# Order within a block of a three-layer graph attention kernel: sums before turnings, weighting before older residuals, first feed-forward product ahead of the next block

## What is computed

```python
for l in range(2):                       # layers 0 and 1
    xn = layernorm(h)
    q, k, v = xn @ wq[l] + bq[l], xn @ wk[l] + bk[l], xn @ wv[l] + bv[l]
    scores = einsum('ehd,ehd->eh', q[dst], k[src]) * scale
    ex = exp(scores - segment_max(scores, dst)[dst])
    agg = segment_sum((ex / segment_sum(ex, dst)[dst])[:, :, None] * v[src], dst)
    h = h + agg @ wo[l] + bo[l]
    h = h + gelu(layernorm(h) @ w1[l] + b1[l]) @ w2[l] + b2[l]
# layer 2 ("typed"): keys are K[src] + 0.2 * rel_w[edge_type]; no feed-forward part
x = layernorm(agg @ Wo + bo + node_features) * gamma + beta
```

## Time and profile before

| | |
|---|---|
| median of 3 runs | 6028.8 us (6025.58 to 6051.66) |
| the profiled execution | 6041.55 us, of which its span is 6039.4 us |
| mean granted TensorE clock | 0.742 of full |
| busy in the span | PE 3256.9 us (54%), DVE 3499.7 us (58%), ACT 1879.4 us (31%), POOL 2782.5 us (46%) |
| layers 0, 1 and typed | about 640 to 2590, 2590 to 4580 and 4580 to 6039 us |

### The profile page before, as it was taken

One profiled execution on the slowest core, in us unless ns is written; L12 is line 12 of the kernel. 1 busy time (PEld: TensorE's weight loads), 2 busy tenths in 40 slices (PEclk: granted clock), 3 DMA queues, 4 the chain that ended last, 5 costly groups with the idle time before them and its releaser, 6 DMA issues. The chain is left out here.

```text
span 6039.4 us, 88354 instructions
## 1 busy us (share of the span) xinstructions
PE 3256.9 (54%) x17373; PEld 2423.7 (40%) x17374; DVE 3499.7 (58%) x5216; ACT 1879.4 (31%) x4257; POOL 2782.5 (46%) x2783
## 2 busy tenths in 40 slices
PE   8575455455555555635545454455565545555655
PEld 6232334333333344523433343333344434444444
DVE  6441445545555555544555555555554758798887
ACT  3342232222222233323222222223334423334444
POOL 0330444544444444244454544444424557777664
PEclk9786677677777777867767777777787767666667
DMA  3343545545455444355554545544434546666654
GB/s 122 120 153 75 160 141 148 158 143 152 140 148 149 143 138 137 102 160 153 149 167 143 158 135 148 152 141 144 138 107 137 162 136 181 183 185 186 176 175 127
DMA packets 369280, 886.73 MB, mean 147 GB/s; under 512 B 140773, under 2 KB 153279, under 8 KB 369225
## 3 DMA queue, kind: packets, MB, share of 16 engines
q0 software_dynamic: 217200, 702.54, 40.3%
q1 hardware_dynamic: 151708, 182.79, 9.4%
q10 hardware_dynamic: 320, 0.84, 0.0%
HBM read 742.87 MB, written 143.30 MB: 147 GB/s over the span
## 5 line engine op out<-in xcount | busy, mean ns | idle before, releaser
L1283 POOL DMA_INDIRECT kv<-kv_dram,idx x2430 | 2421.5, 997 | 1121.8 <-issue 722.1
L2085 PE MATMUL ps_w<-w_ffn,shared 128*128 128x256 f32 x1568 | 567.9, 539 | 1423.8 <-ACT shared L1816 1326.9
L2085 PEld LDWEIGHTS ps_w<-w_ffn,shared 128*128 128x128 f32 x1568 | 432.0, 283 | 1559.5 <-ACT shared L1816 1367.3
L1411 DVE TENSOR_REDUCE sc<-products 128x32 f32<-128x1024 f32 (+2 forms) x654 | 784.3, 1211 | 17.2 <-DVE products L1404 11.8
L1991 PE MATMUL ps_acc<-ident,kv 128*128 128x128 f32 x4944 | 701.9, 305 | 49.0 <-issue 40.0
L1519 DVE TENSOR_TENSOR kv<-kv,ps_q 128x1024 f32<-128x1024 f32 x594 | 683.9, 1215 | 4.5 <-issue 0.3
L1991 PEld LDWEIGHTS ps_acc<-ident,kv 128*128 128x128 f32 x4944 | 645.1, 159 | 96.9 <-issue 69.6
L1816 ACT ACTIVATE shared<-ps_big,b 128x128 f32<-128x128 f32 x784 | 214.6, 380 | 1462.2 <-remote 1444.9
L1404 DVE TENSOR_TENSOR products<-kv,ps_q 128x1024 f32<-128x1024 f32 x436 | 523.4, 1219 | 52.1 <-issue 42.4
L1251 POOL DMA_INDIRECT kv_dram<-rec_out,scatter_to x98 | 100.3, 1024 | 849.3 <-issue 849.3
L2072 PE MATMUL ps_big<-xnaT,w_ffn 128*128 128x128 f32 x3136 | 393.4, 280 | 106.0 <-issue 102.1
(11 more groups left out here) (243 smaller groups left out, 5367.7 us busy)
## 6 DMA issues: line engine op xcount, KB each, us to landing
rec_dram<-rec_out SPq DMA_DIRECT2D x98, 512.0 KB
rec_in<-rec_dram SPq DMA_DIRECT2D x98, 512.0 KB
kv<-kv_dram,idx POOLq DMA_INDIRECT x2430
rec_by_node<-rec_in SPq DMA_DIRECT2D x49, 512.0 KB
windows<-kv SPq DMA_DIRECT2D x49, 384.0 KB
kv_dram<-rec_in SPq DMA_DIRECT2D x49, 256.0 KB
rec_out<-in_x SPq DMA_DIRECT2D x48, 128.0 KB
w_ffn<-in_L_gnn_w SPq DMA_DIRECT2D x4, 1024.0 KB
```

The costliest lines, as they stand in the source:

```text
L1283: pool.indirect_dma_start(kv[:, u * W + slot, :], None, kv_dram[l], bass.IndirectOffsetOnAxis(ap=idx[:, u, slot:slot + 1], axis=0)).then_i ...
L1411: nc.vector.tensor_reduce(scw[:, slice(c * CH * H, (c + 1) * CH * H) if isinstance(c, int) else bass.ds(c * (CH * H), CH * H)].rearrange(" ...
L2085: mm = nc.tensor.matmul(to, gT[:, f, :], w_2[:, f, :], start=False, stop=(f == KF - 1))
```

## The change

On VectorE everything that belongs to older blocks (`older`, which begins with the wait for `f2`, and `scales_of_older`) is moved from ahead of the weighting to behind it, in all three layers. On TensorE `turned_sums` of b goes ahead of `next_q` of b-3 and of the turnings of b-1 and b-2, and `feed_forward` of a block goes from the start of an iteration to the end of the iteration before. No operation is added, removed or resized, and no buffer changes.

```diff
@@ VectorE, iteration @@
                             if exists(b - 2) and not typed:
                                 settle(dve)
                                 row_free(b - 2)
-                        of_older(older)
                         if exists(b):
                             settle(dve)
                             with dve.If(earlier > 0):
...
                             weight_sums(b)
                             even_out(b, k)
-                        of_older(scales_of_older)
                         if exists(b) and first:
                             weigh(k, chunk0, filled)
                         elif exists(b):
                             weigh_last(k, filled)
+                        of_older(older)
+                        of_older(scales_of_older)
@@ TensorE @@
                     def before_sums(b):
                         if exists(b - 2) and not typed:
-                            feed_forward(b - 2)
                             feed_out(b - 2)
...
                             turn_hidden(b - 1)
                         if exists(b - 2) and not typed:
                             turn_normed(b - 2)
+                        if exists(b - 1) and not typed:
+                            feed_forward(b - 1)
...
                             if typed and not last_block(b):
                                 relation_rows(next_round(k))
-                        by_depth(pe, b, deep, beside_weights)
                         if exists(b):
                             turned_sums(k, chunk0, filled)
+                        by_depth(pe, b, deep, beside_weights)
```

## The result

The changed kernel took 5945.09 us (median of 4, 5942.72 to 5957.97) against 6034.43 us before: ratio 0.9856, 95% interval 0.9837 to 0.9875. It is 1.4% faster, where 7.1% was forecast. The profiled execution has a span of 5940.5 us at a granted clock of 0.742, as before.

A forecast was written before the change was run, and what follows sets the result against it. Bound: TensorE signals held until gather bursts drain, then a 15.69 us tail. 6041.55 - 630 (90 blocks x 7.0) + 45 (short bursts) + 40 (layer ends) + 108 (typed) = 5604.6, less 12.7, rounded up to 5600 us; range 5250 to 6150.

The forecast's parts named there:

- the rule: TensorE signals over about 1 to 2 us behind a burst's first gather come late, behind many TensorE instructions at the drain.
- the first half of GELU: Layers 0 and 1: the first product's first half, out by g + 0.1, should be released at once.
- the tail: Layers 0 and 1, after the burst: older work 2.35, root and scales 1.5, record to gather 4.86; 8.7 us against 15.69.
- g: In layers 0 and 1, the start of a burst's first gather, from which the prediction counts its times in us.
- switch of tables: ScalarE's switch to the root's table, now bare: left out of the sum; 1.38 us more a block would add 124 us.
- done by g + 22.3 at the latest: Layers 0 and 1: exponential by g + 16, weights 1.7, weighting 4.61, ending about when the burst drains, so costing nothing.
- rival 2: The first product's second half is caught in a third or so of the blocks: 5750 to 6000 us; chance 0.16.
- rival 3: The second half is caught in all blocks, tail 18.6 us: slower, 6440 us; chance 0.17.
- Sums ahead of turnings: TensorE: sums done by g + 24, query needed at about g + 28; free with 2 us or more in hand.
- Typed layer: Statistics, root and scales behind the weighting delay the next products: +2.1 us a block, +108 us, ends +34 and +200.
- Layer ends: Blocks without a burst, three in each of two layers: some 6.7 us added a block, +40 us, ends 20 and 60.
- Rival 1: The second product's signal isn't held, cycle 27.0 us in place of 38.4: about 5150 us; chance 0.14.

The follow-up runs named there:

- turned_first: Changed kernel with typed layer as before, ScalarE copying the turned rows (xTs1) ahead of the record: 5628.92 us, 0.9317; on another chip 5735.51 us, 0.9361.
- pause_f2: turned_first plus POOL waiting for the second product ahead of its third group of four gathers: 5310.38 us, 0.8775; on another chip 5421.22 us, 0.8858.
- tensor_only: Changed kernel with VectorE's old order put back, so TensorE's part alone: 6260.53 us, 1.0381 against the kernel before.
- query_first: tensor_only with the query's product moved back ahead of the sums, in the set without the hold: 4361.62 us, 1.0044 against the kernel before.
- spaced_loops: Changed kernel with typed layer as before, POOL looping eight empty semaphore steps behind each gather: 8451.09 us, 1.3801 against the kernel before.
- after_third: Changed kernel run again unaltered on another chip: 6209.34 us, 1.0130 against the kernel before.

## Why the prediction was wrong

**Right: the rule, in the sets that have the hold.** Signals of TensorE in a burst come late, the second product's at the drain. turned_first and pause_f2 show it from both sides. But a half that ends just inside a burst comes neither at once nor at the drain, and there the forecast went wrong (below).

**Right: the first half of GELU, and the tail.** The first half starts at g + 1.0. From `second` to the next gather I forecast 8.7 us; it was 4.0 (27.6 to 31.6) + 5.6 = 9.6. The 1.38 us a block for the switch of tables, which the prediction left out of its sum, are not seen: ahead of the block shown above the table load starts at 2024.34, 0.10 us behind VectorE's variance (2024.07 + 0.17), and the root at 2025.64, 0.02 us behind the load's end.

**Wrong: "done by g + 22.3 at the latest ... so the weighting costs nothing as long as the burst lasts".** Two terms of this step were mis-sized, and the larger error is the second. First, the second half was to be released at g + 6 to 12; it came at 12.8 on average (2 to 21 in nearly all blocks), and on later chips at 15.2 and 15.6. I had one block for it. The length of the product is not the reason: it took 5.4 us instead of 3.8 in more than half of the blocks (the granted clock over it was 0.69 in the block shown, and 1.00 over the products of 3.8 us in the earlier trace rows and in turned_first), but in the 31 in which it was short and ended at g + 0.5 to 2.2 the fifth piece came 11.7 us behind its end, in the 33 with an end at g + 3.2 to 4.2 it came 7.8 us behind. In turned_first 80 of 84 products end by g + 0.5, and the fifth piece follows after 1.0 us. Second, GELU's fifth piece to the end of the exponential was to take 3.7 us, a step taken from a block in which it ran behind the burst; inside one it takes 7.3 us (12.8 to 20.1). ScalarE's sequencer instructions (those that handle registers, branches and semaphores ahead of the engine's work) between the two point to why, in the block before the one shown:

```
start    us    ScalarE's sequencer, after
2010.05  0.65  branch
2011.42  0.70  register operations
2012.82  0.70  semaphore
2014.22  0.70  register operations
```

The same kinds take 0.02 to 0.17 us in the 1.4 us before the first of these rows; here they start 1.4 us apart. No run removed this slowness alone, so its share is worked out, not tested. From g + 22.3 to the measured 26.8 it is 0.8 us for the release behind g + 12, 3.6 for the step of 7.3, and 0.1 for the rest. So the weighting outlasts the burst, and `second`, forecast at the drain (22.7), starts at 27.6. The account per block: forecast cycle 31.4, + 4.9 for `second`, + 0.9 of tail = 37.2, as measured. From 39.4 that is 2.2 us saved, not 7.0. The time, 5945 us, lies in the range of rival 2 (5750 to 6000 us, the second half caught in a third of the blocks), but that is luck: the half is late in nearly all blocks, as in rival 3, only by half of a burst instead of a whole one.

turned_first shows that the late release is what makes the step fail: with the second half released at once the exponential ends at g + 11.3, the weighting at g + 17.9, `second` starts at 23.4, and the cycle is 34.2. The 2.8 us that are left over the forecast of 31.4 are 0.7 at `second`, 0.3 from there to `rs1` and 1.8 from `rs1` to the gather.

**Sums ahead of turnings, "nothing gained, nothing lost": right with the weighting first, wrong as a statement on the move itself.** tensor_only showed its price, 7.7 us a block.

**Typed layer: +108 forecast, +70 measured** (1406.7 us before, 1476.6 after), 1.4 us for each of 49 blocks in place of 2.1. **Layer ends: +6.7 us a block forecast, +3.7 measured** (weighting to weighting 24.0 us in one block, 2386.36 to 2410.38, against 20.3 in the earlier trace rows).

**Not foreseen at all:** that the hold isn't always there. Rival 1 (signals free) was priced as a fact still to be found out about this kernel; it differs from set to set, and without the hold the change loses the ground that it was forecast on.

## What to carry to other kernels

When work is moved under a transfer's cover, price each step of it by rows that lie under that cover: 3.7 us outside the burst were 7.3 inside. A gain that hangs on one signal at the boundary of a burst is to be priced by that boundary; moving the product 1 us ahead of it was worth 4%, where the whole change was worth 1.4% at best. And time the kernel before on several chips, before its order is fitted to a wait that may not be there.

## What the hardware showed

- In four of five sets, on four chips, a burst of indirect gathers 1.25 us apart held TensorE's signals: in before the second half of the first product by 16.2 us (median) and up to 23. In one set, at the same pace of gathers, none was held (0.04 us in query_first), and the kernel before took 4343 instead of 6034 to 6130 us. Why stays open.
- The sequencers are slow with it: instructions for registers, branches and semaphores that took over 0.5 us, where most take under 0.1, were 2068 in the trace of before (ScalarE 80, VectorE 502, SyncE 911, POOL 575), and 2 of 32,000 in that of query_first, in the set without the hold. After the change ScalarE has 451 of them, since more of its work lies in the burst.
- With gathers 2.85 us apart both are gone. In the trace of spaced_loops the slow sequencer instructions are 9 of 60,349 in layers 0 and 1, and 465 of 8441 in the typed layer, whose gathers were not spaced; in after_third, on the same chip, they are 1690 of 20,076 and 376 of 8442. ScalarE's waits for "remote" in spaced_loops go the same way, none in layers 0 and 1 and 185 us in the typed layer. So hold and slowness come and go together, within one run too. Whether one makes the other is not shown.
- A pause of 2.65 us in a burst also releases what is held.
- The Trainium skill (Perfetto Trace Analysis, Tensor Engine Instruction) says that the recorded end of a matmul is an estimate and that its semaphore is pushed later, when PSUM has acknowledged. The traces agree, 17.5 us in turned_first; that the gap depends on what the DMA queues do at the time, only the runs here show.
